# One flat list of calls per engine, in a new order, for an attention and mixture-of-experts layer

## What is computed

```python
x = x + attention(layernorm(x), ctx, ctx)      # 8 heads of 16 features
x = x + experts(layernorm(x))

def attention(Q, K, V):
    q, k, v = split(Q @ W_Q.T), split(K @ W_K.T), split(V @ W_V.T)
    scores = einsum('bhqd,bhkd->bhqk', q, k) / sqrt(16)
    attn = softmax(scores, axis=1)             # over the 8 heads
    return merge(einsum('bhqk,bhkd->bhqd', attn, v)) @ W_O.T

def experts(x):                                # 8 experts, the 2 best per token
    logits = x @ Wr + br
    gates = softmax(logits where among the 2 largest, else -inf)
    h = relu(x @ W1[e] + b1[e])                # 256 hidden features
    return sum_e gates[e] * (h @ W2[e] + b2[e])
```

## Time and profile before

| | us |
|---|---|
| median of 3 runs | 210.16 (209.5 to 210.3) |
| span of the profiled execution | 207.8 |
| PE busy | 199.5 (96%) |
| DVE busy | 167.8 (81%) |
| ACT busy | 132.2 (64%) |
| POOL busy | 112.3 (54%) |

### The profile page before, as it was taken

One profiled execution on the slowest core, in us unless ns is written; L12 is line 12 of the kernel. 1 busy time (PEld: TensorE's weight loads), 2 busy tenths in 40 slices (PEclk: granted clock), 3 DMA queues, 4 the chain that ended last, 5 costly groups with the idle time before them and its releaser, 6 DMA issues.

```text
span 207.8 us, 4986 instructions
## 1 busy us (share of the span) xinstructions
PE 199.5 (96%) x1752; PEld 176.5 (85%) x1752; DVE 167.8 (81%) x453; ACT 132.2 (64%) x316; POOL 112.3 (54%) x132
## 2 busy tenths in 40 slices
PE   6999988798999999999999999999999999999995
PEld 6845976686799979997999799998998899789994
DVE  6398769889789999899788988898999888556633
ACT  2236748697568847797677767677757776345441
POOL 8502647869976378629561966376746674010000
PEclk9999999999999999999999999999999999999999
DMA  6649595716515133423140504241000000000000
GB/s 175 160 127 286 153 279 148 224 46 183 158 62 145 69 108 106 103 76 104 41 147 25 170 3 151 57 144 36 0 0 28 0 2 3 25 3 2 25 3 25
DMA packets 20264, 18.70 MB, mean 90 GB/s; under 512 B 1776, under 2 KB 18704, under 8 KB 20240
## 3 DMA queue, kind: packets, MB, share of 16 engines
q1 hardware_dynamic: 17344, 16.85, 28.0%
q10 hardware_dynamic: 2896, 1.54, 2.8%
HBM read 11.83 MB, written 6.55 MB: 88 GB/s over the span
## 4 chain that ended last, share of the span: by engine, by line
PE 91%; DVE 3%; ACT 2%; issue 1%; POOL 1%; POOLq 0%; ACTq 0%; DVEq 0%
PE y_ps L436 28%; PE h_ps L421 22%; PE score_ps L361 7%; PE misc_ps L380 6%; PE score_ps L349 6%; PE h_ps L369 4%; PE score_ps L277 3%; PE misc_ps L401 2%; PE score_ps L338 2%; PE score_ps L421 2%; PE misc_ps L389 2%; PE misc_ps L287 1%; PE misc_ps L327 1%; PE misc_ps L306 1%; PE misc_ps L300 1%
## 5 line engine op out<-in xcount | busy, mean ns | idle before, releaser
L695 ACT ACTIVATE hT<-h_ps,b_sb 128x256 f32<-128x256 f32 x118 | 49.4, 470 | 33.3 <-PE h_ps L421 32.1
L436 PE MATMUL y_ps<-w_sb,hT 128*128 128x128 f32 x508 | 68.0, 277 | 0.0
L436 PEld LDWEIGHTS y_ps<-w_sb,hT 128*128 128x128 f32 x508 | 62.8, 191 | 3.5 <-issue 2.2
L1188 POOL TENSOR_TENSOR half_sum<-e_sb 128x512 f32<-128x512 f32 x28 | 37.3, 1332 | 30.8 <-ACT e_sb L667 30.5
L938 DVE TENSOR_TENSOR attn<-e_sb,e_rcp 128x1024 f32<-128x1024 f32 x32 | 42.1, 1319 | 3.3 <-ACT e_rcp L678 3.3
L930 DVE TENSOR_REDUCE shift_m<-score_ps 128x128 fp32r<-128x1024 f32 x32 | 38.7, 1212 | 2.2 <-PE score_ps L338 1.1
L421 PE MATMUL h_ps<-x1T_hi,w_lo 128*128 128x256 f32 x118 | 37.7, 320 | 1.5 <-ACT hT L695 0.9
L667 ACT ACTIVATE e_sb<-score_ps 128x1024 f32<-128x1024 f32 x32 | 32.8, 1024 | 5.6 <-PE score_ps L361 5.4
L1007 DVE SCALAR_TENSOR_TENSOR acc<-y_ps,gates,acc 128x128 f32<-128x128 f32 x96 | 29.0, 342 | 8.6 <-PE y_ps L436 7.3
L421 PE MATMUL h_ps<-x1T_hi,w_hi 128*128 128x256 f32 x118 | 33.1, 280 | 0.0
L421 PE MATMUL h_ps<-x1T_lo,w_hi 128*128 128x256 f32 x118 | 33.1, 280 | 0.0
(11 more groups left out here) (117 smaller groups left out, 291.3 us busy)
## 6 DMA issues: line engine op xcount, KB each, us to landing
k_scratch<-k_parts SPq DMA_DIRECT2D x14, 256.0 KB, 2.6
k_stack<-k_scratch SPq DMA_DIRECT2D x14, 256.0 KB, 4.0
q_stack<-q_scratch SPq DMA_DIRECT2D x28, 128.0 KB, 2.7
q_scratch<-q_parts SPq DMA_DIRECT2D x7, 256.0 KB, 2.7
w_sb<-in_w SPq DMA_DIRECT2D x1, 1024.0 KB, 6.6
out_y<-y_out SPq DMA_DIRECT2D x7, 128.0 KB, 1.9
x_all<-in_x ACTq DMA_DIRECT2D x1, 768.0 KB, 6.2
ctxT<-in_ctx_t SPq DMA_DIRECT2D x1, 640.0 KB, 6.1
```

Source lines behind the costliest of these rows:

```text
L436: mm = nc.tensor.matmul(product(j, t), hT[:, j % 2, c, t * P:(t + 1) * P], w2_sb[:, e * HC + c, :], start=(c == 0), stop=(c == HC - 1))
L695: op = nc.scalar.activation(hT[:, j % 2, c, :], hidden(j)[:, c * S:(c + 1) * S], ACT.Relu, bias=b1_sb[:, e * HC + c:e * HC + c + 1])
L1188: nc.gpsimd.tensor_tensor(half_sum[:], e[:, 0:HQ // 2], e[:, HQ // 2:HQ], ALU.add).then_inc(sum_step, 1)
```

## The change

All five engine programs are written as one flat list from the first to the last call; `period` and `beginning` are gone. What had been written out in line (the first loads, the constants) became calls as well and was placed in the lists. The calls are the same on each engine, with the same number of each; each waits on the same semaphores with the same counts. Only their order within the engine is new. The two pieces of the diff below are cut from SP and ACT.

```diff
@@ block.sync
-            sp.dma_start(x_all[:, 0:TT, :], x_rows[:, 0:TT, :]).then_inc(x0_in, 16)
-            sp.dma_start(ctxT[:, 0, :], ctx_t[0]).then_inc(ctx_in[0], 16)
+            load_first()
+            load_w1()
             spill_k(1)
-            sp.dma_start(w1_sb[:], w1.rearrange("e d h -> d e h")).then_inc(w1_in, 16)
             load_k_stack(1)
+            spill_k(2)
             spill_q(1)
+            load_k_stack(2)
+            load_w2()
             load_q_stack(1)
...
@@ block.scalar
+            load_w_qkvo()
+            load_tables()
+            load_ctx(1)
+            load_x1()
+            load_ctx(2)
+            load_x_rest()
+            take_xnT(0)
+            take_k_first()
+            take_k_hi(1)
+            split_w1(0)
+            load_small()
+            take_k_hi(2)
+            exponentiate(0, 0)
```

More of the change, by code:

```diff
@@ new lines, in _ @@
+            subtract_max(1, 3)
+            fill(4)
+            subtract_max(2, 0)
+            route(0, x1T_lo_made, 1)
+            expert_up(0, 0)
+            expert_up(0, 1)
+            scores(2, 1)
+            project_k(3, logits_made, 1)
+            expert_down(0, 0)
+            scores(2, 2)
+            expert_down(0, 1)
+            subtract_max(2, 1)
+            transpose_xn(3, k_lo_made, 3)
+            expert_up(0, 2)
+            expert_up(0, 3)
+            project_q(3, xnT_taken, 4)
@@ new lines, in _ @@
+            gated_b2(2, k_lo_made, 6)
+            expert_up(2, 6)
+            transpose_xn(6, b2_added, 3)
+            expert_down(2, 5)
+            transpose_x1n(3, xnT_taken, 7)
+            scores(5, 1)
+            expert_up(2, 7)
+            expert_up(3, 0)
+            subtract_max(5, 0)
+            expert_down(2, 6)
+            expert_down(2, 7)
+            route(3, x1T_lo_made, 4)
+            expert_up(3, 1)
+            subtract_max(5, 1)
+            project_q(6, logits_made, 4)
@@ new lines, in _ @@
+            subtract_max(5, 3)
+            gated_b2(3, k_lo_made, 7)
+            expert_up(3, 6)
+            transpose_xn(7, b2_added, 4)
+            scores(6, 0)
+            scores(6, 1)
+            expert_down(3, 5)
+            transpose_x1n(4, xnT_taken, 8)
+            expert_up(3, 7)
+            subtract_max(6, 0)
+            route(4, x1T_lo_made, 5)
+            expert_up(4, 0)
+            expert_down(3, 6)
+            expert_down(3, 7)
+            project_q(7, logits_made, 5)
@@ new lines, in _ @@
+            load_ctx(2)
[7 more added lines that the diff above has]
+            exponentiate(0, 0)
+            split_w1(1)
+            split_w1(2)
+            invert_sum(0, 0)
+            exponentiate(0, 1)
+            split_w1(3)
+            take_xnT(1)
+            take_q_hi(1)
+            make_xn(2)
+            take_v(0)
+            take_xnT(2)
@@ new lines, in _ @@
+            exponentiate(2, 0)
+            relu(0, 0)
+            gap_power(0)
+            take_k_hi(3)
+            invert_sum(1, 1)
+            relu(0, 1)
+            make_xn(3)
+            invert_sum(1, 2)
+            take_xnT(3)
+            split_w1(6)
+            relu(0, 2)
+            take_q_hi(3)
+            invert_sum(1, 3)
+            relu(0, 3)
+            relu(0, 4)
+            make_xn(4)
+            take_heads(1)
+            exponentiate(2, 1)
+            relu(0, 5)
```

1290 lines of the change are left out of this document (758 added, 532 removed).

## The result

The changed kernel took **351.2 us** (median of 4 runs, 348.8 to 352.2) against 209.8 of the kernel before on the same chip: 1.673 times as long, 95% interval 1.666 to 1.679. The forecast was 292 with a range of 268 to 312. The sign was right, the size was not, and the time lies outside the range by 39 us.

The account below looks back on a forecast made before the run. PE was taken as the bound: 194.8 us for its work, start and end, plus waits of 35.8, 25.3, 18.7, 4.8 and 5.7 make 285.1. The median's offset gives 287.5, clock falls add 4.8: forecast 292, range 268 to 312.

Parts of the forecast that it names:

- What bounds the kernel: Whole kernel: PE bounds it with 188.4 us of own work; a new order can win at most part of 13 us.
- I follow the new lists by hand: Whole kernel: the five new lists walked wait by wait with old durations; sum 285.1 us before median and clock.
- VectorE's hold on `expert_down`: `expert_down` calls on PE wait for `add_expert`, late in VectorE's list: 27.0 us with (0,5).
- on `attend_values`: `attend_values` on PE waits for the last `normalize` of its batch on VectorE: 22.3 us with batch 0.
- the pairs of `expert_up`: With one `h_ps`, a second `expert_up` waits for the first's relu on ScalarE: 8.1 us in all.
- the sum of PE's own work: All PE calls times their cost when nothing holds them: 188.4 us.
- the smaller waits up to `scores(3,0)`: PE waits after `scores(1,0)`: `attend_values(0)` 3.6 us, three `expert_up` 3.3, `expert_down(0,5)` 1.7, eight smaller ones 4.6.
- hidden by a later one: Before `scores(4,0)`: the same spill and load pattern as before `scores(3,0)`, taken to add nothing.
- `scores(1,0)`: First `scores` of batch 1 waits for q through DRAM: 8.3 us on PE, start about 36.
- `transpose_xn(1)`: At the start PE idles 5.1 us because ScalarE's small loads, behind w1, delay its k copy and VectorE's layer norm.
- Four falls at 1.2: 4.8: PE's clock falls in four of ten gaps of 3 us or more, adding 4.8 us; bounds 0 and 23.
- The rival of a fall in every long gap: PE's clock falls in all ten long gaps at 2.3 us each: 310 us, chance 0.13.

Follow-up runs that it names:

- the fillers: The changed kernel with filler products, which compute nothing, on PE ahead of twenty calls that wait; 329.1 us against 351.2.
- the repaired kernel: The changed kernel with 30 calls moved on GpSimd, SP, PE and VectorE (memset, q loads, `expert_up` pairs, `add_expert`, `normalize`, w1 split); 282.8 us.

## Why the prediction was right or wrong

- **What bounds the kernel, and the sign: right.** PE was busy 96% of the time, so an order could win little and lose whatever PE newly waits for. The best order found here wins 0.3%.
- **"I follow the new lists by hand": right for what VectorE and PE do to one another.** The terms for VectorE's hold on `expert_down` and on `attend_values`, and the pairs of `expert_up`, came out within 4 us each (31.0 for 27.0, 20.7 for 22.3, 9.0 for 8.1), the wait before `expert_down(1,1)` at 4.7 for 5.0, before the last `attend_values` at 5.8 for 5.7; the largest single miss among them is `expert_down(4,0)`, 5.5 for 3.0. The repairs on the chip gave most of them back, and they added up. (In the sum of PE's own work 64 x 0.89 + 64 x 0.71 is 102.4 and 32 x 0.48 is 15.4, 0.8 us more than stated; nothing rests on it.)
- **The step that failed first: the smaller waits up to `scores(3,0)`, which had no term for `scores(2,0)`.** The sum took the start as SP's, ScalarE's and VectorE's matter. GpSimd's list was read for its work, and not for what it releases. `zero_q_stack(0)`, which SP's load of q for batch 2 waits for, moved behind `ln2_end(0)`: 14.1 us. In the kernel before it runs at 8.87 us and nobody waits for it, so no wait in the old trace names it. The splits of w1 are the same kind, 4.5 together. And the transfer before `scores(4,0)`, "hidden by a later one" in the walk, was not hidden: 4.1. On the other hand the walk gave `scores(3,0)` 6.1, and it waited 3.1.
- **`scores(1,0)`: right in kind, 2 us short.** Walked 8.3 and a start at 36; it waited 10.2 and started at 39.75. The spill left at 27.99 (walked 26.8), and the four loads took 3.28 us to issue behind w2's, not 1.8. With w2 moved away they took 1.98.
- **`transpose_xn(1)`: near in size, wrong reason.** 5.1 walked through ScalarE's loads, 3.4 measured behind VectorE's own queue; taking the loads away changed nothing. That the size was near is luck.
- **The clock: the term that was mis-sized.** "Four falls at 1.2: 4.8", bounds 0 and 23. There were 14, and they added 35.5 us of work. Both factors failed, the count by 14 to 4 and the price by 2.5 to 1.2: in a stretch at low clock PE works 5.1 us on the mean, 8.3 at most, and half of that is added. I had the upper bound of the price about right (2.3), and took half of it without a row that said so. The count was made over ten gaps of 3 us or more, of which four were taken; the fall at 54.0 follows a wait of 2.9, and the one at 190.5 waits of 2.3 and 1.5, at `expert_down(2,3)` and the next `expert_down`. What shows in the time is less, 22 us, and with that the term was still 17 too small. "HAM oscillation", of the page "TensorE: Matmul & The Clock Gate" of the Trainium skill, says that a kernel with repeated waits pays at each. The trace agrees with it in kind, with 14 falls. The rival of a fall in every long gap (310) was nearer than the forecast, at a chance of 0.13; its ten falls at 2.3 make 23, close to the 22 that the fillers gave back, though from fewer falls than there were.
- **The range.** Its upper end held the clock's bound and no wait that had not been found. Such waits came to 23 us here (14.1 and 4.5 behind GpSimd, 4.1 before `scores(4,0)`); a walk of five lists with some 800 calls leaves some out, and each adds on the same side.

## What to carry to other kernels

When instructions move, list for each engine not only what it computes but what it releases (a zeroed buffer, a split weight, a freed bank), and look at how far each of these moved: here the places of 11 `add_expert` and 6 `normalize` cost 36 us and that of one memset 11, on engines that were busy half of the time or less. Where PE's order is tight, new waits add up nearly one by one, and the long ones also lower the clock, at some 22 us in 141 here. Fillers give part of that back where they are no longer than the wait; where they were longer, they made the kernel 28.5 us slower. Engines' lists are a set: taken back on two engines alone, the old order lost another 7 us.

## What was not expected of the hardware

- **VectorE's xn waits for GpSimd's memset.** Two records of 0.60 us took 2.01, 3.76 and 2.15 beside memsets of 1.80 each, and 0.60 again when these were moved. Not every instruction waits: beside a memset the BATCH_NORM_STATS2 kept its 0.47 us, while the TENSOR_SCALAR of ln_var took 0.87 in place of 0.17. The Trainium skill, page "SBUF — State Buffer", section "SBUF: two separate sides", says that the two engines share a pair of ports, which one instruction holds to its end while the other is fully blocked, and that of VectorE's instructions this concerns those in a two-port mode and, in some cases, those with two inputs in SBUF. The durations agree with it; in which mode an instruction ran, no trace shows. In the kernel before and in the change both xn run clear of the long memsets. But the old trace did show such a wait, in its first microseconds, where VectorE makes `neg_ident` beside two memsets:

```profile
1.59 3.69 DVE L1157 TENSOR_SCALAR neg_ident<-ident 128x128 fp32r<-128x128 f32 x1 [1.59 <-POOL ident L1255]
1.65 1.81 POOL L1259 MEMSET q_stack<- 128x2048 f32 x1
...
3.40 1.81 POOL L1260 MEMSET v_pad<- 128x2048 f32 x1
```

  The same record takes 0.22 us in the change, at 10.83, with no memset beside it.
- **A DMA issue can take longer than its own 0.45 us.** The four loads of q take 1.74 to 1.98 us to issue, and 3.28 and 4.03 right behind the issue of w2's load. ScalarE's issue of the first small load took 2.87 us beside the early w1, against 1.23 and 1.18 with w1 later.
- **Slowed work is paid only in part.** Of 38.7 us by which PE's work was longer, fillers gave 22 back in the change; of about 19 they gave 3.7 in the repaired kernel.
